# New orders of the units of work on each engine in a fused kernel of attentions and expert layers

## What is computed

```python
x = x + xattn(layernorm(x), ctx)  # causal self attention, norm, attention over 257 context rows, norm, relu layer, norm
x = x + attn(layernorm(x))        # 16 heads of 32, causal softmax times a decay matrix, projection
x = x + ffn(layernorm(x))         # silu(x1) * x2, norm, sw3; rows picked by an index also pass the best of 8 experts
```

## Time and profile before

| | us |
|---|---|
| median of three runs | 1449.03 |
| the profiled execution, span | 1452.8 |
| PE busy in it | 1365.6 (94%) |
| DVE busy | 1128.1 (78%) |
| ACT busy | 601.9 (41%) |
| POOL busy | 526.1 (36%) |
| DMA queue q1, share of 16 engines | 38.3% |

### The profile page before, as it was taken

One profiled execution on the slowest core, in us unless ns is written; L12 is line 12 of the kernel. 1 busy time (PEld: TensorE's weight loads), 2 busy tenths in 40 slices (PEclk: granted clock), 3 DMA queues, 4 the chain that ended last, 5 costly groups with the idle time before them and its releaser, 6 DMA issues.

```text
span 1452.8 us, 33270 instructions
## 1 busy us (share of the span) xinstructions
PE 1365.6 (94%) x13860; PEld 851.7 (59%) x13861; DVE 1128.1 (78%) x2335; ACT 601.9 (41%) x1147; POOL 526.1 (36%) x545
## 2 busy tenths in 40 slices
PE   7679999999999999999999999999999999998888
PEld 3355566666656666665665656666665666655443
DVE  6787777777787877778778877777778877777776
ACT  2544444443444444343434444444444444443222
POOL 0133333433444333443443333343443433343222
PEclk9899999999999999999999999999999999999899
DMA  9732444433333444433333344443333344434440
GB/s 349 259 131 74 146 146 146 144 123 105 133 112 115 146 146 146 146 137 101 122 130 105 139 146 146 146 142 114 111 138 105 123 146 146 147 134 161 149 161 30
DMA packets 38662, 201.41 MB, mean 139 GB/s; under 512 B 5096, under 2 KB 5992, under 8 KB 28400
## 3 DMA queue, kind: packets, MB, share of 16 engines
q1 hardware_dynamic: 37648, 198.93, 38.3%
q10 hardware_dynamic: 864, 0.36, 0.1%
HBM read 182.24 MB, written 17.04 MB: 137 GB/s over the span
## 4 chain that ended last, share of the span: by engine, by line
PE 70%; DVE 19%; POOL 4%; ACT 4%; issue 3%; DMA 0%; DVEq 0%; POOLq 0%; ACTq 0%; SPq 0%
PE ps_a L1716 11%; PE ps_a L1739 8%; PE ps_t L1739 7%; PE ps_t L1703 6%; PE ps_a L1725 6%; PE ps_a L1751 4%; PE ps_a L1783 4%; POOL rstd L636 4%; PE ps_t L1716 3%; PE ps_v L1716 3%; DVE stats L1178 3%; DVE arena L1309 3%; PE ps_t L1826 2%; PE ps_t L1775 2%; PE ps_t L1751 2%
## 5 line engine op out<-in xcount | busy, mean ns | idle before, releaser
L645 POOL TENSOR_TENSOR act_l<-act_t,act_h 128x512 f16<-128x512 f32 (+1 forms) x176 | 199.5, 1134 | 351.4 <-ACT act_t L789 199.4
L636 POOL TENSOR_TENSOR rstd<-var,mhalf 128x1 f32<-128x1 f32 x224 | 181.8, 812 | 333.7 <-DVE var L1180 328.9
L781 ACT ACTIVATE act_h<-ps_t,scale 128x512 f16<-128x512 f32 (+1 forms) x110 | 70.8, 644 | 206.2 <-PE ps_t L1703 206.2
L645 POOL TENSOR_TENSOR last_slot<-last_slot 128x512 f16<-128x512 f32 x80 | 90.0, 1125 | 156.7 <-ACT last_slot L789 90.8
L1739 PE MATMUL ps_a<-act_h,arena 128*128 128x128 f16 x1408 | 87.6, 221 | 17.3 <-ACT act_h L781 17.3
L1739 PEld LDWEIGHTS ps_a<-act_h,arena 128*128 128x128 f16 x1408 | 81.9, 99 | 28.3 <-ACT act_h L781 21.3
L789 ACT ACTIVATE act_t<-ps_t,scale 128x512 f32<-128x512 f32 (+1 forms) x110 | 70.3, 639 | 49.1 <-PE ps_t L1703 49.1
L1739 PE MATMUL ps_t<-act_h,arena 128*128 128x128 f16 x1408 | 87.0, 221 | 3.3 <-ACT act_h L781 3.3
L1716 PE MATMUL ps_a<-arena,act_h 128*128 128x512 f16 x352 | 83.6, 380 | 1.9 <-ACT act_h L781 1.9
L1309 DVE TENSOR_SCALAR arena<-ps_a,unscale 32x512 f32<-32x512 f32 x64 | 48.2, 753 | 47.0 <-PE ps_a L1751 45.8
L1739 PEld LDWEIGHTS ps_t<-act_h,arena 128*128 128x128 f16 x1408 | 81.4, 99 | 4.9 <-DVE arena L1037 2.4
(11 more groups left out here) (380 smaller groups left out, 3150.7 us busy)
## 6 DMA issues: line engine op xcount, KB each, us to landing
arena<-in_ctx_t SPq DMA_DIRECT2D x32, 2056.0 KB, 8.4
arena<-in_ctx_n SPq DMA_DIRECT2D x32, 2048.0 KB
ctx_last<-in_ctx_last SPq DMA_DIRECT2D x32, 256.0 KB
arena<-in_ew SPq DMA_DIRECT2D x8, 1024.0 KB, 6.3
x_in<-in_x SPq DMA_DIRECT2D x22, 256.0 KB, 7.3
x_scratch<-rows SPq DMA_DIRECT2D x22, 256.0 KB, 8.8
out<-rows SPq DMA_DIRECT2D x22, 256.0 KB, 2.1
arena<-in_ew SPq DMA_DIRECT2D x8, 512.0 KB, 7.2
```

Of the source, the lines that this page charges most:

```text
L636: nc.gpsimd.tensor_tensor(rstd[s][:], var[s][:], mhalf[:], ALU.pow).then_inc(rstd_ready[s], 1)
L645: nc.gpsimd.tensor_tensor(act_l[s][:, chunks], act_t[s][:, chunks], act_h[s][:, chunks], ALU.subtract).then_inc(act_l_ready[s], 1)
L781: nc.scalar.activation(act_h[s][:, 0:width // P].rearrange("p c r -> p (c r)"), bank[s][:, 0:width], ACT.Copy, scale=scale[:, k:k + 1]).th ...
```

## The change

Only the three tables differ: no unit, wait, buffer or transfer is added or taken away. The lags of whole lists are shifted too where a list now starts at another unit; what counts is the order that results.

- Middle rounds, PE: `self_mix, project_out, turn_h2, project_out_l` becomes `self_mix, turn_h2, project_out, project_out_l`, for the `turn_h2` of tiles 3 to 28.
- Middle rounds, DVE: `context_scores` moves from between `ffn_in` and `silu` to behind `z_norm`; `context_total` from behind `xn_moments` to ahead of `ffn_out`; `context_mix` ahead of `head_scores`.
- Middle rounds, ACT: `turn_z_t` ahead of `turn_z`; `turn_xn, context_sum, turn_xn_t, context_scaled, head_scores` in place of `turn_xn_t, turn_xn, context_sum, head_scores, context_scaled`; `project_v` ahead of `self_scores`. POOL: nothing.
- Start, PE: `set_04, set_05, set_06` ahead of `turn_xn` of tile 0; `value_self_l, self_scores, set_08, set_09` in place of `set_08, self_scores, set_09, value_self_l`. DVE: `set_01, set_02, xn_moments, set_03, turn_xn` in place of `xn_moments, set_01, turn_xn, set_02, set_03`; `set_09` ahead of `self_mix`; `set_15` to `set_20` each one to three units later. ACT: `turn_xn, turn_xn_t` ahead of `set_3`; `project_query` ahead of `set_9`; `context_scores` ahead of `set_wcv`, `set_w12`; `set_wk, set_wq, set_wv` together behind `turn_h2` of tile 0. From tile 0 on, PE's `project_k_l` ahead of `ffn_out`.
- End, PE: `head_mix` ahead of `turn_p`, `turn_h2` between `project_out` and `project_out_l`, `project_query_l` ahead of `turn_x2n`, `ffn_in` ahead of `context_scores`, `project_q_l` and `turn_pc` ahead of `ffn_out`; `e_in0` behind `head_mix` of tile 30, `e_in1` and `e_in2` each a few units later, `e_out0` and `e_zt1` behind `head_scores` of tile 31, `e_in4` behind everything. DVE: `head_scores` of tile 30 ahead of `e_moments`, that of tile 31 ahead of `e_zn1`, `e_bias2` and `e_z2`; `e_z3` and `e_zn3` behind `x2_norm` of tile 31.

The lines of the diff in which these stand:

```diff
 FIRST = {
-    "pe": [(3, "turn_z"), (3, "ffn_out"), (1, "set_13"), (3, "ffn_out_l"), (0, "set_01"), (2, "project_q_l"),
-        (1, "turn_pc"), (0, "set_02"), (0, "set_03"), (2, "project_k_l"), (2, "project_v"), (0, "turn_xn"),
-        (0, "set_04"), (0, "set_05"), (0, "set_06"), (1, "context_mix"), (2, "head_scores"), (2, "project_v_l"),
...
+    "pe": [(1, "project_query_l"), (3, "ffn_in"), (1, "context_scores"), (0, "set_01"), (2, "set_21"), (3, "ffn_in_l"),
+        (2, "turn_x1n"), (2, "project_k"), (2, "project_q"), (0, "set_02"), (0, "set_03"), (0, "set_04"),
...
+        (0, "turn_xn"), (1, "context_mix"), (2, "head_scores"), (0, "set_07"), (0, "project_self"),
...
-    "dve": [(3, "z_norm"), (3, "ffn_out"), (1, "set_14"), (0, "xn_moments"), (0, "set_01"), (0, "turn_xn"),
-        (2, "project_k"), (0, "set_02"), (0, "set_03"), (0, "set_04"), (1, "set_14b"), (1, "set_15"),
-        (1, "context_mix"), (2, "head_scores"), (1, "context_total"), (1, "set_16"), (1, "context_scaled"),
...
-        (0, "set_07"), (1, "set_18"), (1, "context_out"), (0, "self_scores"), (0, "set_08"), (1, "context_norm"),
-        (2, "project_out"), (1, "set_19"), (0, "self_mix"), (3, "set_23"), (0, "self_norm"), (0, "set_09"),
...
+    "dve": [(2, "set_18"), (0, "set_01"), (3, "x2_norm"), (2, "hidden"), (1, "set_10"), (2, "out_norm"), (1, "set_11"),
+        (2, "x1_norm"), (3, "ffn_in"), (3, "silu"), (0, "set_02"), (1, "set_12"), (2, "set_19"), (3, "z_norm"),
+        (1, "set_13"), (1, "context_scores"), (2, "set_20"), (3, "ffn_out"), (0, "xn_moments"), (0, "set_03"),
...
+        (1, "set_15"), (0, "set_05"), (2, "head_total"), (0, "set_06"), (0, "project_self"), (1, "set_16"),
...
-    "act": [(2, "turn_x1n"), (1, "set_w12"), (0, "set_1"), (3, "ffn_in"), (0, "set_2"), (2, "turn_x1n_t"),
-        (3, "turn_z"), (3, "turn_z_t"), (1, "context_scores"), (0, "set_3"), (2, "project_q"), (1, "set_w3"),
-        (1, "turn_pc"), (2, "project_k"), (0, "turn_xn_t"), (0, "turn_xn"), (1, "set_wproj"), (1, "context_sum"),
...
-        (1, "turn_w"), (0, "set_5"), (1, "turn_w_t"), (1, "set_wk"), (1, "set_wq"), (2, "head_mix_t"),
-        (2, "head_mix"), (0, "self_scores"), (0, "value_self"), (0, "turn_p"), (0, "set_6"), (0, "set_7"),
...
-        (0, "set_9"), (2, "turn_x2n"), (1, "set_wv"), (0, "project_query"), (0, "set_wcv")],
+    "act": [(2, "turn_h2"), (2, "turn_h2_t"), (1, "set_8"), (2, "set_wk"), (2, "set_wq"), (0, "set_1"), (2, "set_wv"),
...
+        (2, "turn_x1n"), (3, "ffn_in"), (1, "set_9"), (2, "turn_x1n_t"), (3, "turn_z"), (3, "turn_z_t"),
+        (1, "context_scores"), (2, "project_k"), (1, "set_wcv"), (1, "turn_pc"), (2, "project_v"),
+        (2, "project_q"), (0, "turn_xn"), (0, "turn_xn_t"), (0, "set_3"), (1, "set_w12"), (1, "context_sum"),
...
+        (0, "set_6"), (1, "set_wproj"), (0, "value_self"), (0, "turn_p"), (0, "set_7")],
 ORDER = {
...
-        (2, "head_mix"), (0, "self_mix"), (2, "project_out"), (1, "turn_h2"), (2, "project_out_l"), (1, "hidden"),
...
+        (0, "turn_p"), (2, "head_mix"), (0, "self_mix"), (1, "turn_h2"), (2, "project_out"),
+        (2, "project_out_l"), (1, "hidden"), (1, "hidden_l"), (0, "turn_h"), (2, "turn_x2n"),
...
-    "dve": [(3, "z_norm"), (2, "project_k"), (3, "ffn_out"), (0, "xn_moments"), (1, "context_total"), (0, "turn_xn"),
-        (2, "head_scores"), (1, "context_mix"), (1, "context_scaled"), (2, "head_total"), (0, "project_self"),
...
-        (2, "ffn_in"), (0, "context_scores"), (2, "silu")],
...
+        (3, "silu"), (3, "z_norm"), (1, "context_scores"), (2, "project_k"), (1, "context_total"),
+        (3, "ffn_out"), (0, "xn_moments"), (0, "turn_xn"), (1, "context_mix"), (2, "head_scores"),
...
-    "act": [(3, "turn_x2n_t"), (2, "turn_x1n"), (3, "ffn_in"), (2, "turn_x1n_t"), (3, "turn_z"), (3, "turn_z_t"),
-        (1, "context_scores"), (2, "project_k"), (1, "turn_pc"), (2, "project_q"), (0, "turn_xn_t"), (0, "turn_xn"),
-        (1, "context_sum"), (2, "head_scores"), (1, "context_scaled"), (0, "project_self"), (1, "turn_w"),
...
+        (3, "ffn_in"), (2, "turn_x1n_t"), (3, "turn_z_t"), (3, "turn_z"), (1, "context_scores"),
+        (2, "project_k"), (1, "turn_pc"), (2, "project_q"), (0, "turn_xn"), (1, "context_sum"),
+        (0, "turn_xn_t"), (1, "context_scaled"), (2, "head_scores"), (0, "project_self"), (1, "turn_w"),
...
 LAST = {
-    "pe": [(2, "project_q"), (3, "e_in4"), (3, "turn_z"), (2, "project_k_l"), (3, "ffn_out"), (3, "ffn_out_l"),
-        (1, "turn_pc"), (2, "project_q_l"), (2, "e_zt1"), (1, "context_mix"), (2, "head_scores"), (2, "e_in3"),
...
-        (1, "e_turn"), (0, "project_self_l"), (1, "e_logits"), (0, "value_self"), (1, "e_in0"), (0, "self_scores"),
...
-        (1, "e_in1"), (0, "self_mix"), (2, "e_out2"), (2, "project_out"), (2, "project_out_l"), (1, "e_zt0"),
-        (2, "e_zt3"), (2, "e_out3"), (1, "turn_h2"), (1, "hidden"), (0, "turn_h"), (1, "hidden_l"), (1, "e_in2"),
...
+        (2, "project_query"), (2, "project_query_l"), (4, "turn_x2n"), (3, "e_zt0"), (4, "ffn_in"),
+        (2, "context_scores"), (4, "ffn_in_l"), (3, "turn_x1n"), (4, "e_zt3"), (4, "e_out3"), (3, "e_in2"),
...
+        (2, "turn_pc"), (4, "ffn_out"), (4, "ffn_out_l"), (2, "context_mix"), (3, "head_scores"),
+        (3, "project_v"), (1, "turn_xn"), (3, "project_v_l"), (1, "project_self"), (2, "e_turn"),
+        (1, "project_self_l"), (2, "e_logits"), (2, "turn_w"), (3, "e_out0"), (3, "e_zt1"), (1, "value_self"),
...
+        (3, "head_mix"), (2, "e_in0"), (1, "turn_p"), (3, "e_out1"), (1, "self_mix"), (3, "project_out"),
+        (2, "turn_h2"), (3, "project_out_l"), (4, "e_in4")],
...
-        (1, "context_scores"), (3, "silu"), (3, "z_norm"), (3, "e_total"), (2, "e_zn1"), (2, "e_bias2"),
-        (2, "project_k"), (3, "ffn_out"), (0, "xn_moments"), (2, "e_z2"), (0, "turn_xn"), (1, "context_mix"),
...
+        (3, "head_scores"), (3, "e_zn1"), (2, "e_moments"), (2, "context_scaled"), (3, "e_bias2"),
...
+        (3, "e_z2"), (2, "e_gate_b"), (1, "self_scores"), (2, "context_out"), (2, "context_norm"),
...
+        (2, "e_z0"), (3, "project_out"), (2, "e_zn0"), (3, "x2_norm")],
```

## The result

The changed kernel takes 1474.25 us in the median of five executions (1471.05 to 1480.18), the kernel before 1449.14 beside it (1448.67 to 1452.83): a ratio of 1.0182, 95% interval [1.016, 1.0204]. The forecast was slower, at 1456.2 with a range to 1463; the time is 25.1 us above the kernel before and lies outside. The profiled execution of the changed kernel spans 1477.3 us against 1452.8.

A forecast was written before the change was run, and what follows sets the result against it. TensorE, busy 94% of the span, was taken as the bound. Middle +10.7 and +2.4, start +1.9, end -7.8 sum to +7.2 us, added to the 1449.0 median: 1456.2 forecast, range 1446 to 1463.

The forecast's parts named there:

- the largest term: Middle, PE: `turn_h2` ahead of `project_out` waits for `context_norm`, 0.41 us a round, 10.7 us lost in 26 rounds.
- the rival that half is absorbed: PE's 0.33 wait before `turn_x2n` absorbs most of the swap; 0.08 a round stays, 1447.6 us; chance 0.17.
- the one that the norm comes in time: Middle: `context_norm` ends 0.36 earlier, so the swap costs nothing, 1445.5 us; chance 0.15 with other faster ways.
- Cover claimed for `context_scaled` and `head_scores`: Middle: these reorderings cost nothing, since DVE's L1204 waits 0.52 for PE anyway; without that cover 0.2 a round.
- The rest of the middle: Middle exchanges on ACT and DVE besides the PE swap: together 0.09 a round, 2.4 us in 26 rounds.
- The 0.05 of `turn_z_t`: Middle, ACT: `turn_z_t` ahead of `turn_z` makes `ffn_out` 0.20 late, of which 0.05 is left at `ffn_out_l`.
- The first step: Start: `xn_moments` behind `set_02` and `set_06` ahead of `turn_xn` delay the chain; tile 0's `self_mix` at 48.5, +4.6 us.
- The steps behind it: Start, later: 2.7 us come back at `context_scores`, another 1.0 lost before tile 2's `project_self`, -1.0 up to tile 3.
- the start is not caught up: Start: the +4.6 stays and idle PE falls to 1.2 GHz again, 3 us more, 1459 to 1462; chance 0.13.
- The failed step: Rounds under `LAST`: other tiles' units between dependent pairs shorten rounds from 43.6 to 41.2 us, 2 x 2.4 = -4.8.
- The +1.7 for the loop's first row: End: `e_in4` now stands behind everything and the loop's first DVE row waits for it, +1.7 us.
- The slow spell in the tail: Last stretch: low clock follows the wait before `e_turn`, so moving `e_in0` saves nothing; otherwise 3.0 us less.

The follow-up runs named there:

- best: Kernel before plus new start without orders up to tile 0's `self_mix`, new end, six POOL waits, `e_in4` ahead of last `turn_z`: 1447.10 us, ratio 0.9973.
- end_new: Kernel before with only the rounds from tile 29 on in the new order: 1453.87 us, ratio 1.0021.

## Why the prediction was right and wrong

**Right in sign and in the largest term.** `turn_h2` behind `context_norm` was forecast at 0.41 a round and measured at 0.40, with the queue behind it moved as described; the rival that half is absorbed, and the one that the norm comes in time, are out. Cover claimed for `context_scaled` and `head_scores` held: L1206 still waits 0.46 in the new order.

**The rest of the middle was mis-sized**, 0.09 a round against 0.20. The 0.05 of `turn_z_t` was right. For `context_total` ahead of `xn_moments` the text had 0.08 to 0.15 and a PE without slack, and then entered 0.04 in the sum; 0.15 was measured. Cost: 2.5 us.

**The start: +1.9 forecast, +6.4 measured in the fastest executions.** The first step had the order right: transposes at 31.61 (about 31 forecast), the end of `set_3` at 35.4 (34.7 forecast). That these times come near is partly luck: `set_05` came at 25.63 and not at 26.7, and `set_06` took 5.40 and not the 3.70 of the old order. It left out what PE's clock does behind the waits that the new order makes: the cross products `set_06` and `set_10` last 5.40 and 5.22 us, where the one at the old order's full clock takes 3.60 or 3.70, the first behind a wait of 3.21, the second behind 1.20 and 0.71.

```profile
25.63 0.82 PE L1650 MATMUL ps_e<-rows,p_t 128*32 128x32 bf16 x32 [3.21 <-DVE p_t L1068]
26.38 5.40 PE L1665 MATMUL ps_v<-arena 128*128 128x512 f32 x8
31.61 0.60 PE L1705 MATMUL ps_t<-ident,rows 128*128 128x128 f32 x4
...
44.19 5.22 PE L1665 MATMUL ps_a<-arena 128*128 128x512 f32 x8
...
50.92 1.13 PE L1777 MATMUL ps_t<-v_n,p_t 128*128 128x512 f32 x2 [1.40 <-ACT p_t L828]
```

It also left out that ACT's copy of `v_n` now stands behind one of `set_10`'s product, so that the wait in front of `self_mix` is 1.40 and not 0.35. Together +7.0 instead of +4.6. The steps behind it were forecast at -2.7 and came to +1.3: the 2.5 us won up to tile 1 (41.6 a round instead of 44.2) go again in the next (46.6 instead of 42.2), where `set_18` stands ahead of `hidden`; moving it behind won nothing in the total, since `project_k` needs what it makes. The rival "the start is not caught up" (1459 to 1462) described this part best; it was given 0.13.

**The end: -7.8 forecast, nothing measured.** The failed step is "the new order puts another tile's unit between each pair; what stays is 0.4 ..., 0.7 ... and 0.4 ...: 41.2 a round". It looked at PE's pairs alone and took DVE's rows at the durations of the old order. The exchanges on POOL put each subtraction right behind the `rstd` that releases a norm, and 2.6 us of lengthened norms made DVE the bound of these rounds. With the norms kept apart the round is 41.97, 0.8 over the forecast. That is a second, smaller miss of the same step: the old order has three waits of 0.78 in such a round and the text lists two; the third, in front of `project_k` (1289.96 in the kernel before), stays in the new order. The trace of the kernel before had a sign of the lengthening: in its rounds under `LAST`, L1184 lasts 1.37 behind a subtraction too.

```profile
1278.02 1.37 DVE L1184 TENSOR_SCALAR rows<-rows,mv,rstd 128x512 f32<-128x512 f32 x1 [0.44 <-POOL rstd L636]
```

Up to `head_mix` of tile 31 the gain was 2.6 of the 7.1 forecast from `self_mix` of tile 31 on (2.4 of them for the second round under `LAST`), 3.4 with the norms apart (4.9 in `best`). The +1.7 for the loop's first row was right in place and near in size (+2.0), but not by `e_in4` alone: with `e_in4` put back the row is as late (24.2). That `e_zt3` and `e_out3`, now in front of the last `turn_z`, hold it is read from the rows and was not run.

**The slow spell in the tail** went where it was expected: in the old order it made `e_in0` 6.71 us long, in the new one it makes `context_out`, the first product behind the wait before `e_turn`, 3.60 long instead of 1.89 and `context_out_l` 1.82 instead of 1.03, and `e_in0` takes 3.70. 3.0 us were lost to low clock there and 2.5 are now: moving `e_in0` saved next to nothing, as the sum had it.

```profile
1374.99 1.03 PE L1837 MATMUL ps_t<-ident,last_slot 128*128 128x128 f32 x4 [2.50 <-DVE last_slot L1457]
...
1380.32 3.60 PE L1718 MATMUL ps_a<-arena,act_h 128*128 128x512 f16 x8 [0.68 <-ACT act_h L806]
...
1386.47 3.70 PE L1871 MATMUL ps_a<-arena,last_slot 128*128 128x512 f32 x8
```

The rule cited there from the Trainium skill, "TensorE: Matmul & The Clock Gate" (Part 1: The HAM clock gate), that the clock follows how busy the array has been, agrees with these rows. It would also have spoken for low clock behind the new wait at `set_05`, where it was not applied.

**What the terms leave.** 10.4 + 4.9 for the middle, 6.4 for the start and 0 for the end make 21.7, against 22.8 in the fastest execution and 25.1 in the median of the changed kernel. The 2 to 3 us between the two are executions with more at low clock; that the changed kernel has more of it is measured (mean clocks of 0.984 to 0.990 against 0.988 to 0.992 for the kernel before), why is open.

## What to carry to other kernels

When an order is changed, look at which instructions of DVE and POOL will then start together, and not only at who waits for whom: a norm released by POOL and a POOL instruction queued right behind the releasing one met in both rounds of every kernel with this order, and waits on POOL that parted them won more than the new order of the end did by itself. In a steady round an exchange that adds 0.4 us costs it in each round if the wait behind it is released by the delayed engine itself; read that releaser before crediting slack. At a start or an end, price each new wait of PE with the low clock that can follow it as well.

## What the runs showed of the hardware

- **DVE and POOL exclude each other.** 128x512 norms of 0.75 and 0.55 us become 1.57 to 1.69 and 1.37, a 128x1 row of 0.22 becomes 0.94, POOL's subtraction of 1.16 becomes 1.67 when it comes second; statistics with one input that start inside a subtraction keep their 0.69 or 0.70 (88 rows of the changed kernel). Parting them by waits brought back 2.03 us in the first of two rounds, and 2.04 in the second up to `e_turn`.
- **The same holds for POOL's `rstd`, in both orders.** In the changed kernel it lasts 0.55 us where no DVE row with two inputs in SBUF is running (64 rows), 0.73 beside one of 128x256 (30) and 0.98 or 0.99 beside one of 128x512 (117), such as the product with `gamma` that each of these norms makes in the meantime. The norm waits for it, so this stands on DVE's chain; no run moved it.
- **The granted clock is not a property of the program alone.** The stretch from `self_mix` of tile 31 to the end, in the old order, took 134.9 us in one profile (mean clock 0.97) and 138.6 in another (0.95); the changed kernel's five executions lie 9 us apart, at mean clocks from 0.990 (1471.05) to 0.984 (1480.18). Behind an idle spell of PE the next product took 3.24 us in one kernel and 3.60 in another (`context_out` in `end_new` and in the changed kernel) where it takes 1.89 at 2.4 GHz. So a change of 0.3% was read here from ten executions, with the fastest one beside the median.
